# GpSimd's bias adds in the dense stages, moved to VectorE at the head of each trip of the edge sums

## The chip, the cores and the metric

The kernel runs on one core of a Trainium2 chip, in one launch. The metric is the device time of that core in microseconds. Engines are named as the profile does: PE is TensorE (PEld its weight loads), DVE is VectorE, ACT is ScalarE, POOL is GpSimd, SP is SyncE.

## The reference

A graph network on N = 3125 nodes with D = 256 features and 50000 edges. Eight layers follow each other, each x = x + f(layernorm(x)), where f is in turn a sparse sum, a mixture of experts, two graph attention layers, experts, a graph convolution with a small MLP, experts, two SAGE layers, experts. Cut to the four places where the change adds something:

```python
# L1_gnn: two attention layers; the second ends with "+ b2" (gat2)
h1 = relu(gat_conv(x, src, dst, W1, att_src1, att_dst1, b1, n))
out = gat_conv(h1, src, dst, W2, att_src2, att_dst2, b2, n)
# L2_gnn: sum over edges, then an MLP whose second bias is b2 (gcn2)
h7 = segment_sum(msgs, row_sl) + b
out = relu(h7 @ W1 + b1) @ W2 + b2
# L3_gnn: two SAGE layers with biases b1 (sage1) and b2 (sage2)
def _sage_conv(x, src, dst, W_l, b_l, W_r):
    mean_nb = segment_sum(take(x, src), dst) / maximum(deg, 1)
    return mean_nb @ W_l + b_l + x @ W_r
h = _sage_conv(relu(_sage_conv(x, src, dst, W1_l, b1, W1_r)), src, dst, W2_l, b2, W2_r)
```

## The kernel before

The nodes lie in 25 row tiles of 128 (NT = 25). X, in SBUF, holds the running x as [128, NT, 256] in f32; acc holds the result of an edge sum in the same layout with some columns more; TR holds the part of a SAGE layer that comes from the node itself (x @ W_r).

A layer on the graph is made of two kinds of stage. `dense(...)` is a stage between sums: for each group of row tiles (`FIVES` is five groups of 5 tiles, `SHORT_END` is 5, 5, 5, 5, 3, 2) VectorE takes over what came before (`front`, or rows that land from the experts, `got`), makes the layernorm (`stats`, and `finish`, whose L865 writes the normalised rows XN), TensorE transposes the rows and multiplies them with a weight, ScalarE copies the products, and SyncE stores a table in DRAM. `edge_sum(...)` then gathers rows of that table, one of 128 edges per instruction, on GpSimd (L1063, an indirect DMA); VectorE builds a 0/1 matrix S for each 128 edges (L1153, L1155), TensorE multiplies S with the gathered rows G into a product buffer psM (L1138), and VectorE adds that product to the row tile of acc to which these edges belong (`add_up`, L1169). The loop over edge tiles runs on each engine by itself, with semaphores between them: 26 trips of 16 tiles in the sums of this text. At the head of a trip VectorE loads the 16 tile numbers from SBUF into registers (L1199) and computes semaphore thresholds (L1166). The ring of G has 4 groups of 4 tiles, so the gathers run ahead of the rest.

The stages in order, as far as they matter here: gat2's sum (2051 to 2600 us), the dense stage of ffn1 (to 2666), experts; gcn's sum (2946 to 3495), the dense stage of gatf (to 3589); later the dense stage of sage1, sage1's sum (4670 to 5204), the dense stage of sage2, sage2's sum, the dense stage of ffn3. A dense stage is one block: all engines meet at its end (L642).

GpSimd, which has no other work in a dense stage but a maximum over partitions in some, adds there what doesn't come out of a matmul. With `pool_front` it starts at the block's start and VectorE waits for it group by group (semaphore `pooled`): in ffn1 it adds the row gat2 to X (L1806), in gatf the row gcn2 to X (L1827), 5 instructions of 128x1280 each. With `pool_back` it waits until a group's products have been copied (semaphore `kept`): in sage1 it adds the row sage1 to TR (L1886) and the row sage2 to X (L1887), in sage2 TR to X (L1890). In ffn1 VectorE's `front` is L1734, acc times the reciprocal of the denominators, and L1793, X plus acc; in gatf its first operations are L849.

## Time and profile before

| | |
|---|---|
| median of 3 runs | 6393.6 us (6387.85 to 6398.09) |
| the profiled execution, its own time | 6414.7 us |
| its span, mean granted TensorE clock | 6413.0 us, 0.815 |
| busy: PE, DVE, ACT, POOL | 4584.1 (71%), 3483.9 (54%), 2388.4 (37%), 3812.5 (59%) us |

Busy us of the engines by stage, from the windows of the trace:

| stage | window, us | PE | DVE | ACT | POOL | clock |
|---|---|---|---|---|---|---|
| gat2's sum | 2051 to 2600 | 431.29 | 321.79 | 497.34 | 405.76 | 0.83 |
| dense, ffn1 | 2600 to 2666 | 30.46 | 43.77 | 11.56 | 17.97 | 0.50 |
| gcn's sum | 2946 to 3495 | 411.13 | 470.66 | 279.41 | 403.09 | 0.98 |
| dense, gatf | 3495 to 3589 | 74.96 | 44.61 | 35.53 | 16.60 | 0.84 |
| dense, sage1 | 4566 to 4667 | 58.30 | 51.00 | 26.03 | 29.30 | 0.78 |
| sage1's sum | 4670 to 5204 | 309.62 | 270.08 | 20.10 | 394.96 | 0.76 |
| dense, sage2 | 5206 to 5268 | 52.56 | 15.87 | 23.76 | 14.45 | 0.92 |

A row of the groups by line reads: line, engine, operation, what is written from what, shapes, count; then busy time and mean duration in ns; then the idle time of the engine just before these instructions, with what ended it and how much of the idle time each ended. "issue" is an end that the profile shows no cause for. The clock is the share of TensorE's full clock that was granted.

### The profile page before, as it was taken

To read this page: it belongs to the slowest core of one execution; us is meant where nothing else is said; L and a number is where in the kernel's file an instruction comes from. 1 tells how busy PE (TensorE), PEld (TensorE's weight loads), DVE (VectorE), ACT (ScalarE), POOL (GpSimd) and SP (SyncE) were. 2 spreads that over 40 slices of the span, in tenths; PEclk is the share of its full clock that TensorE was granted. 3 is DMA by queue.
4 is the path that set the end of the run, shared out by engine and by line. 5 is a ranking of instruction groups with operands and counts; after the bars stand their busy time and mean duration, and the time that the engine had idled before them with its cause. 6 is when DMAs were issued, how large, how long until landed. Compare 5 with 4: busy or idle time off the path is not lost. (4 is left out here: it accounts for less than half of the span.)

```text
span 6413.0 us, 102638 instructions
## 1 busy us (share of the span) xinstructions
PE 4584.1 (71%) x20814; PEld 3576.9 (56%) x20815; DVE 3483.9 (54%) x11701; ACT 2388.4 (37%) x8150; POOL 3812.5 (59%) x3882
## 2 busy tenths in 40 slices
PE   3846664967887887477777888868755565556997
PEld 1434443756666666465555788867533433335876
DVE  7877876245554555638887444452455445554012
ACT  0745540228997999224554211112200010001221
POOL 4757751756775777364776477754377747771221
PEclk8989986988887888698999655559877777776998
DMA  2023332133333333333333111122233333333555
GB/s 54 1 83 103 103 89 78 58 89 99 106 106 85 106 106 106 79 102 119 103 104 75 23 8 8 8 22 78 85 95 105 105 76 105 105 105 99 178 175 172
DMA packets 303001, 562.12 MB, mean 88 GB/s; under 512 B 87704, under 2 KB 181570, under 8 KB 302530
## 3 DMA queue, kind: packets, MB, share of 16 engines
q0 software_dynamic: 169952, 401.65, 25.0%
q1 hardware_dynamic: 119852, 146.38, 7.1%
q10 hardware_dynamic: 13110, 13.08, 0.6%
q8 instruction: 36, 0.59, 0.0%
q14 instruction: 51, 0.42, 0.0%
HBM read 491.05 MB, written 69.80 MB: 87 GB/s over the span
## 5 line engine op out<-in xcount | busy, mean ns | idle before, releaser
L1138 PE MATMUL psM<-G,S 128*128 128x257 f32 (+3 forms) x6080 | 1939.8, 456 | 998.3 <-DMA G<-table_ones,ids 604.2
L1138 PEld LDWEIGHTS psM<-G,S 128*128 128x128 f32 x6080 | 1329.4, 251 | 1426.3 <-DVE acc L1169 640.8
L1169 DVE TENSOR_TENSOR acc<-acc,psM 128x257 f32 (+3 forms) x3068 | 1151.2, 375 | 1012.5 <-PE psM L1138 820.5
L1063 POOL DMA_INDIRECT G<-table_ones,ids x1248 | 1196.9, 959 | 430.3 <-issue 355.4
L1063 POOL DMA_INDIRECT G<-table_gat,ids x840 | 811.8, 966 | 266.1 <-issue 255.1
L1021 ACT ACTIVATE G<-G 128x64 f32<-128x64 f32 x3360 | 824.7, 333 | 6.8
L1063 POOL DMA_INDIRECT G<-table_ffn_gat,ids x548 | 522.5, 954 | 176.2 <-issue 141.5
L1517 POOL DMA_INDIRECT out_by_choice<-ys,to_choice x248 | 248.6, 1002 | 526.7 <-DVE ys L1637 471.2
L1637 DVE TENSOR_TENSOR ys<-psY,b2b 128x256 f32<-128x256 f32 x248 | 105.2, 425 | 801.1 <-PE psY L1576 744.3
L1063 POOL DMA_INDIRECT G<-table_gcn,ids x416 | 402.5, 968 | 197.1 <-issue 125.6
L1090 PEld LDWEIGHTS psE<-AD,St 128*128 128x128 f32 x2800 | 504.2, 260 | 27.1 <-issue 6.3
L1576 PE MATMUL psY<-w2s,Ht 128*128 (+1 forms) x2240 | 504.0, 379 | 0.0
L1100 PE MATMUL psV<-Ot,Pk 128*128 128x272 f16 (+1 forms) x2496 | 483.3, 303 | 0.0
L1090 PE MATMUL psE<-AD,St 128*128 x2800 | 479.5, 299 | 4.6 <-ACT St L1014 4.6
L1610 ACT ACTIVATE Ht<-psH,b1t 128x256 f32<-128x256 f32 x560 | 260.8, 474 | 584.9 <-PE psH L1564 584.3
L1010 ACT CAST ids<-id_by_dst 128x4 int32 (+1 forms) x428 | 78.6, 185 | 1032.1 <-PE psM L1138 1006.9
L1576 PEld LDWEIGHTS psY<-w2s,Ht 128*128 128x128 f32 x2240 | 426.3, 190 | 58.6 <-issue 0.4
L1153 DVE TENSOR_SCALAR S<-iota_row,dl_by_dst 128x128 f32<-128x128 f32 x1712 | 450.2, 296 | 2.1 <-issue 0.5
L1512 POOL DMA_INDIRECT XN<-rows_by_token,from_token x184 | 179.5, 975 | 357.0 <-POOLq L1277 301.9
L1081 PE MATMUL psS<-ident,S 128*128 128x128 f32 x1400 | 292.0, 346 | 78.9 <-DVE S L1153 74.0
L1100 PEld LDWEIGHTS psV<-Ot,Pk 128*128 128x128 f16 x2496 | 247.5, 99 | 141.4 <-issue 6.3
L1178 DVE TENSOR_TENSOR z<-G,psE 128x16 f32<-128x16 f32 x347 | 59.3, 171 | 478.7 <-DMA G<-table_ffn_gat,ids 265.5
(380 smaller groups left out, 6570.3 us busy)
## 6 DMA issues: line engine op xcount, KB each, us to landing
w1s<-in_L_ffn_W SPq DMA_DIRECT2D x32, 1024.0 KB, 8.5
w2s<-in_L_ffn_W SPq DMA_DIRECT2D x32, 1024.0 KB
G<-table_ones,ids POOLq DMA_INDIRECT x1248, 2.8
land<-out_by_choice SPq DMA_DIRECT2D x75, 256.0 KB, 3.1
G<-table_gat,ids POOLq DMA_INDIRECT x840
rows_by_token<-XN SPq DMA_DIRECT2D x20, 640.0 KB, 3.3
G<-table_ffn_gat,ids POOLq DMA_INDIRECT x548, 2.4
G<-table_gcn,ids POOLq DMA_INDIRECT x416
```

What stands on the lines that cost most here:

```text
L1021: m = nc.scalar.activation(part, part, ACT.Copy, scale=G[:, g, j, HEADS * c + h:HEADS * c + h + 1])
L1063: pool.indirect_dma_start(G[:, g, j, :], None, table, bass.IndirectOffsetOnAxis(ids[:, g, j:j + 1], 0)).then_inc(gathered[g], 16)
L1081: m = nc.tensor.transpose(psS[:, k0 % 2, j * P:(j + 1) * P], S[:, g, j, :], ident[:, :])
L1090: m = nc.tensor.matmul(psE[:, k0 % 2, j, :], St[:, g, j, :], AD[:, bass.ds(bl[j], 1), :].rearrange("p a h -> p (a h)"), start=True, stop=True)
L1100: m = nc.tensor.matmul(psV[:, k, v, 0:HW], Pk[:, ring, k, :], Ot[:, ring, v * HW:(v + 1) * HW], start=False, stop=False)
L1138: nc.tensor.matmul(psM[:, j, 0:W], S[:, g, j, :], G[:, g, j, :], start=True, stop=True).then_inc(summed, 1)
L1153: m = nc.vector.tensor_scalar(S[:, k0 % GB, j, :], iota_row[:, :], DL[:, t], None, ALU.is_equal)
L1169: nc.vector.tensor_tensor(ab, ab, psM[:, n0 % EG, 0:W], ALU.add).then_inc(added, 1)
L1512: pool.indirect_dma_start(xs[:, n % XR, h, :], None, XD, bass.IndirectOffsetOnAxis(from_token[:, n * HALVES + h:n * HALVES + h + 1], 0)).t ...
L1517: pool.indirect_dma_start(YD, bass.IndirectOffsetOnAxis(to_choice[:, n * HALVES + h:n * HALVES + h + 1], 0), ys[:, n % 2, h, :], None).the ...
L1576: m = nc.tensor.matmul(psY[:, q, 0:D], Ht[:, s, h, q * P:(q + 1) * P], w, start=(h == 0), stop=(h == nh - 1))
L1610: nc.scalar.activation(Ht[:, s, h, :], psH[:, h % 2, 0:TT], func, bias=b1t[:, bass.ds(e, 1), h:h + 1].rearrange("p a h -> p (a h)")).then_ ...
```

## The change

`pool_front`, `pool_back` and `pooled` go from `dense`, and with them the 27 additions that GpSimd made in the dense stages (5 in ffn1, 5 in gatf, 12 in sage1, 5 in sage2). `edge_sum` gets a parameter `each`: on VectorE, at the head of each of the 26 trips, behind the load of the 16 tile numbers and ahead of the first group, `each(i)` adds to row tile i. In gat2's sum it adds the row gat2 to tile i of X, in gcn's the row gcn2 to tile i of X, in sage1's the row sage1 to tile i of TR and the row sage2 to tile i of X, in sage2's tile i of TR to tile i of X: 26, 26, 52 and 26 instructions of 128x256. As there are 26 trips and 25 tiles, X and TR get a 26th tile that nobody reads; GpSimd zeroes it in X at the start, and VectorE in TR at the head of sage1's sum (`zeros_beside`).

```diff
@@ def dense
-                        if pool_front is not None:
-                            for t0, t1 in groups:
-                                pool_front(t0, t1).then_inc(pooled, 1)
-                        if beside is not None:
-                            beside(pool)
-                        if pool_back is not None:
-                            for t0, t1 in groups:
-                                pool.wait_ge(kept, t1)
-                                pool_back(t0, t1).then_inc(pooled, 1)
...
                             if front is not None:
-                                if pool_front is not None:
-                                    dve.wait_ge(pooled, g + 1)
                                 m = front(link, t0, t1)
@@ def edge_sum
                                 skip_runtime_bounds_check_because="the chip clamps the block to the last one")
+                            if each is not None:
+                                each(i)
                             for g in range(GB):
@@
+        def tile_of(v, i):
+            return v[:, bass.ds(i, 1), :].rearrange("p a d -> p (a d)")
+
+        def add_to(v, w):
+
+            return nc.vector.tensor_tensor(v, v, w, ALU.add)
@@ gat2's sum and ffn1
-            edge_sum("gat2", LB, tabg[1], WGAT, acc, self_terms(XN, own, acc, 64), AD=AD, c=64)
-
-            def add_gat2(t0, t1):
-                return nc.gpsimd.tensor_tensor(X[:, t0:t1, :], X[:, t0:t1, :], wide(row["gat2"][:, :], t1 - t0), ALU.add)
-            dense("ffn1", FIVES, xn_row, fold=denominators, front=divided_into_x, pool_front=add_gat2, small=(wgt["gate1"], 8, LG, []), tables=[(XD, XN, D, "rows")])
+            edge_sum("gat2", LB, tabg[1], WGAT, acc, self_terms(XN, own, acc, 64), AD=AD, c=64,
+                     each=lambda i: add_to(tile_of(X, i), row["gat2"][:, :]))
+            dense("ffn1", FIVES, xn_row, fold=denominators, front=divided_into_x, small=(wgt["gate1"], 8, LG, []), tables=[(XD, XN, D, "rows")])
@@ sage1 and sage2
-            def add_biases(t0, t1):
-                nc.gpsimd.tensor_tensor(TR[:, t0:t1, :], TR[:, t0:t1, :], wide(row["sage1"][:, :], t1 - t0), ALU.add)
-                return nc.gpsimd.tensor_tensor(X[:, t0:t1, :], X[:, t0:t1, :], wide(row["sage2"][:, :], t1 - t0), ALU.add)
-
-            def add_own(t0, t1):
-                return nc.gpsimd.tensor_tensor(X[:, t0:t1, :], X[:, t0:t1, :], TR[:, t0:t1, :], ALU.add)
+            def add_biases(i):
+                add_to(tile_of(TR, i), row["sage1"][:, :])
+                return add_to(tile_of(X, i), row["sage2"][:, :])
+
+            def add_own(i):
+                return add_to(tile_of(X, i), tile_of(TR, i))
+
+            def zeros_beside(acc, W):
+                def begin():
+                    nc.vector.memset(TR[:, NT, :], 0.0)
+                    return nc.vector.memset(acc[:, :, 0:W], 0.0)
+                return begin
@@
-            edge_sum("sage1", LB, tab1[1], W1TAB, acc, zeros_in(acc, W1TAB))
+            edge_sum("sage1", LB, tab1[1], W1TAB, acc, zeros_beside(acc, W1TAB), each=add_biases)
-            edge_sum("sage2", LB, tab1[2], W1TAB, acc, zeros_in(acc, W1TAB))
+            edge_sum("sage2", LB, tab1[2], W1TAB, acc, zeros_in(acc, W1TAB), each=add_own)
```

The same is done to gcn's sum and gatf with the row gcn2, and the sizes of X and TR become NT + 1 tiles.

On GpSimd, between the last gathers of gat2's sum and the first gathers of ffn1's experts, there stands before (L1806 is the addition of the row gat2; ISA in front of it is a configuration instruction):

```order
L1063 DMA G<-table_gat,ids 128x260 x4
L993 UNCONDITIONAL_BRANCH
L665 UNCONDITIONAL_BRANCH
L1806 ISA
L1806 TENSOR_TENSOR X<-X,row_gat_1 128x1280 x5
L642 UNCONDITIONAL_BRANCH
L1508 UNCONDITIONAL_BRANCH
L1512 DMA xs<-rows_by_token,from_token 128x256 x10
```

and now, with lines numbered as in the changed kernel:

```order
L1053 REGISTER_ALU
L1053 COMPARE_AND_BRANCH
L1050 DMA G<-table_gat,ids 128x260 x4
L980 UNCONDITIONAL_BRANCH
L665 UNCONDITIONAL_BRANCH
L1497 UNCONDITIONAL_BRANCH
L1501 DMA xs<-rows_by_token,from_token 128x256 x10
```

The configuration instruction and the five additions are gone, and GpSimd passes the dense stage with nothing to do.

On GpSimd in the dense stage of sage1 there stands before, for each group, a pair of additions; this is its beginning, behind the scatters of the experts:

```order
L1477 UNCONDITIONAL_BRANCH
L665 UNCONDITIONAL_BRANCH
L1886 ISA
L1886 TENSOR_TENSOR TR<-TR,row_sage_1 128x1280
L1887 TENSOR_TENSOR X<-X,row_sage_1 128x1280
```

and now the gathers of the sum follow directly:

```order
L1466 UNCONDITIONAL_BRANCH
L665 UNCONDITIONAL_BRANCH
L1046 UNCONDITIONAL_BRANCH
L1053 UNCONDITIONAL_BRANCH
L1053 ISA
L1050 DMA G<-table_ones,ids 128x257 x4
```

All twelve additions have left this place.

On VectorE, at the head of the loop of sage1's sum, there stands before (L1719 zeroes acc, L1169 adds a product to it, L1153 builds S):

```order
L1719 MEMSET acc 128x6425
L1198 UNCONDITIONAL_BRANCH
L1198 ISA
L1199 TENSOR_LOAD blk_by_dst
L1166 REGISTER_ALU
L1167 REGISTER_ALU
L1169 ISA
L1169 TENSOR_TENSOR acc<-acc,psM 128x257
```

and now:

```order
L1885 MEMSET TR 128x256
L1886 MEMSET acc 128x6425
L1185 UNCONDITIONAL_BRANCH
L1185 ISA
L1186 TENSOR_LOAD blk_by_dst
L1712 ISA
L1712 TENSOR_TENSOR TR<-TR,row_sage_1 128x256
L1712 REGISTER_ALU
L1712 TENSOR_TENSOR X<-X,row_sage_1 128x256
L1153 REGISTER_ALU
L1154 REGISTER_ALU
L1156 ISA
L1156 TENSOR_TENSOR acc<-acc,psM 128x257
```

The two additions stand between the load of the tile numbers and the first addition of a product; the threshold registers come behind them.

## Rows read from the trace of the kernel before

**Rows 1.** The groups by line, GpSimd, in gat2's (2051 to 2600), gcn's and sage1's sums.

```profile
L1063 POOL DMA_INDIRECT G<-table_gat,ids x420 | 405.8, 966 | 133.5 <-issue 127.7 <-ACT ids L1010 5.8
...
L1063 POOL DMA_INDIRECT G<-table_gcn,ids x416 | 402.5, 968 | 197.1 <-issue 125.6 <-SPq L993 70.6 <-ACT ids L1010 0.9
...
L1063 POOL DMA_INDIRECT G<-table_ones,ids x416 | 395.0, 949 | 131.0 <-issue 124.7 <-ACT ids L1010 6.3
```

**Rows 2.** The same view, VectorE, in gcn's sum (2946 to 3495).

```profile
L1169 DVE TENSOR_TENSOR acc<-acc,psM 128x256 f32 x420 | 171.7, 409 | 75.9 <-PE psM L1138 75.8
```

**Rows 3.** The timeline of ffn1's dense stage: start us, us, engine, instruction, [idle before].

```profile
2606.14 17.97 POOL L1806 TENSOR_TENSOR X<-X,row_gat 128x1280 f32<-128x1280 f32 x5 [21.59 <-issue]
...
2598.82 0.78 DVE L1784 RECIPROCAL rden<-acc 128x100 f32<-128x100 f32 x1 [1.08 <-PEq L993]
2609.11 4.09 DVE L1734 TENSOR_TENSOR acc<-acc,rden 128x1280 f32<-128x1280 f32 x1 [9.51 <-POOL X L1806]
2613.24 4.05 DVE L1793 TENSOR_TENSOR X<-X,acc 128x1280 f32<-128x1280 f32 x1
...
2619.45 1.93 DVE L1734 TENSOR_TENSOR acc<-acc,rden 128x1280 f32<-128x1280 f32 x1
...
2629.44 1.48 DVE L1734 TENSOR_TENSOR acc<-acc,rden 128x1280 f32<-128x1280 f32 x1
2630.95 1.49 DVE L1793 TENSOR_TENSOR X<-X,acc 128x1280 f32<-128x1280 f32 x1
```

**Rows 4.** The timeline of gatf's dense stage.

```profile
3496.36 6.37 DVE L849 TENSOR_TENSOR acc<-acc,DINV 128x1280 f32<-128x1280 f32 x2
...
3498.78 1.09 PE L687 MATMUL psA<-ident,acc 128*128 128x128 f32 x4 [2.53 <-DVE acc L849]
```

**Rows 5.** The timeline of sage1's dense stage, VectorE.

```profile
4599.29 1.70 DVE L865 TENSOR_SCALAR XN<-X,mv,rstd 128x256 f32<-128x256 f32 x5
...
4610.65 2.95 DVE L865 TENSOR_SCALAR XN<-X,mv,rstd 128x256 f32<-128x256 f32 x5
...
4637.23 2.30 DVE L865 TENSOR_SCALAR XN<-X,mv,rstd 128x256 f32<-128x256 f32 x3
...
4647.53 5.01 DVE L865 TENSOR_SCALAR XN<-X,mv,rstd 128x256 f32<-128x256 f32 x2
```

**Rows 6.** The same stretch, TensorE.

```profile
4601.32 1.88 PE L728 MATMUL psL<-w_sage,xts 128*128 128x512 f32 x4
...
4614.14 3.08 PE L728 MATMUL psL<-w_sage,xts 128*128 128x512 f32 x4
...
4652.60 0.69 PE L719 MATMUL psT<-ident,XN 128*128 128x128 f32 x2 [5.29 <-DVE XN L865]
4653.08 3.62 PE L728 MATMUL psL<-w_sage,xts 128*128 128x512 f32 x4
```

**Rows 7.** The end of sage2's dense stage: GpSimd's timeline, and the last table store.

```profile
5260.41 2.88 POOL L1890 TENSOR_TENSOR X<-X,TR 128x1280 f32<-128x1280 f32 x1 [5.86 <-ACT XN L802]
...
L662 SPq DMA_DIRECT2D table_ones<-XN x1: 360/360/360, 5260.4 to 5260.4; - x1
...
DMA to landing us min/median/max: 4.5/4.5/4.5
```

**Rows 8.** The timeline at the head of gat1's sum.

```profile
1461.04 7.09 DVE L1725 TENSOR_TENSOR acc<-XN,own 128x1280 f32<-128x1280 f32 x5
1461.50 7.45 POOL L1063 DMA_INDIRECT G<-table_gat,ids  x1 [0.30 <-issue]
```

**Rows 9.** Register steps of line L1166, and the gathers that start beside them.

```profile
L1166 DVEq ALU_OP  x1: 40/40/40, 3214.7 to 3214.7; - x1
...
3214.82 0.95 POOL L1063 DMA_INDIRECT G<-table_gcn,ids  x1 [0.30 <-issue]
...
L1166 DVEq ALU_OP  x1: 40/40/40, 4912.4 to 4912.4; - x1
...
4912.46 0.95 POOL L1063 DMA_INDIRECT G<-table_ones,ids  x1 [0.30 <-issue]
```

More of the change, by code:

```diff
@@ L117, in linker @@
             return link
-        X = sb("X", [P, NT, D])
+        X = sb("X", [P, NT + 1, D])
         ident = sb("ident", [P, P])
@@ L460, in _ @@
                         nc.gpsimd.memset(zeros[:, :], 0.0).then_inc(zeroed, 1)
-                        nc.gpsimd.memset(X[:, NT - 1, :], 0.0).then_inc(own, 1)
+                        nc.gpsimd.memset(X[:, NT - 1:NT + 1, :].rearrange("p t d -> p (t d)"), 0.0).then_inc(own, 1)
                         nc.gpsimd.memset(eps[:, :], LN_EPS).then_inc(own, 1)
@@ L593, in dense @@
         def dense(name, groups, rows, ln=True, got=None, front=None, first=None, col=None, W=None, scale=None, into=None,
-                  small=None, tables=(), att=None, fold=None, degrees=None, beside=None, pool_front=None, pool_back=None, also=None):
+                  small=None, tables=(), att=None, fold=None, degrees=None, also=None):
             LAG = 9 if first is not None else 0
@@ L899, in _ @@
                             if front is not None:
-                                if pool_front is not None:
-                                    dve.wait_ge(pooled, g + 1)
                                 m = front(link, t0, t1)
@@ L946, in _, with edge_sum @@
                             nc.vector.tensor_tensor(zo[:, :, :], zo[:, :, :], att.AD[:, :, HEADS:2 * HEADS], ALU.subtract).then_inc(scored, 1)
-        def edge_sum(name, e, table, W, acc, begin, AD=None, c=64, job=None):
+        def edge_sum(name, e, table, W, acc, begin, AD=None, c=64, job=None, each=None):
             with ExitStack() as ctx:
@@ L1823, in program @@
             edge_sum("gcn", LA, tabx, D, acc, lambda: nc.vector.tensor_copy(acc[:, :, :], XN[:, :, 0:D]),
-                     job=Job(LF, LF.by_pool, list_dram[LF.name][0:LF.slots, :]))
-            def add_gcn2(t0, t1):
-                return nc.gpsimd.tensor_tensor(X[:, t0:t1, :], X[:, t0:t1, :], wide(row["gcn2"][:, :], t1 - t0), ALU.add)
+                     job=Job(LF, LF.by_pool, list_dram[LF.name][0:LF.slots, :]), each=lambda i: add_to(tile_of(X, i), row["gcn2"][:, :]))
             def to_x(t, ps):
@@ L1831, in program @@
             dense("gatf", FIVES, xn_row, first=First(acc_row2, acc_group, DINV, column["gcn"], (wgt["gcn1"], column["gcn1"]), wgt["gcn2"], to_x, None),
-                  pool_front=add_gcn2, small=(wgt["gatf"], WF + HEADS, TF, []), att=Att(TF, AD, own, 4), tables=[(XD, XN, D, "rows"), (tabf, TF, WF, "small")])
+                  small=(wgt["gatf"], WF + HEADS, TF, []), att=Att(TF, AD, own, 4), tables=[(XD, XN, D, "rows"), (tabf, TF, WF, "small")])
             edge_sum("gatf", LF, tabf, WF, acc, self_terms(TF, own, acc, 4), AD=AD, c=4)
@@ L1873, in program @@
             sb, pb, sem = scope(ctx)
-            TR = sb("TR", [P, NT, D])
+            TR = sb("TR", [P, NT + 1, D])
             acc = sb("acc", [P, NT, W1TAB])
@@ L1903, in joined_into_x @@
                 return m
-            dense("sage1", SHORT_END, xn_row, got=True, W=(wgt["sage1"], 2 * D), into=own_row, also=xn_row, pool_back=add_biases, tables=[(tab1[1], XN, D, "kept")])
-            edge_sum("sage1", LB, tab1[1], W1TAB, acc, zeros_in(acc, W1TAB))
-            dense("sage2", FIVES, xn_row, ln=False, fold=in_degrees, front=joined, pool_back=add_own,
+            dense("sage1", SHORT_END, xn_row, got=True, W=(wgt["sage1"], 2 * D), into=own_row, also=xn_row, tables=[(tab1[1], XN, D, "kept")])
+            edge_sum("sage1", LB, tab1[1], W1TAB, acc, zeros_beside(acc, W1TAB), each=add_biases)
+            dense("sage2", FIVES, xn_row, ln=False, fold=in_degrees, front=joined,
                   W=(wgt["sage2"], 2 * D), into=own_row, also=xn_row, tables=[(tab1[2], XN, D, "kept")])
-            edge_sum("sage2", LB, tab1[2], W1TAB, acc, zeros_in(acc, W1TAB))
+            edge_sum("sage2", LB, tab1[2], W1TAB, acc, zeros_in(acc, W1TAB), each=add_own)
             dense("ffn3", FIVES, xn_row, fold=in_degrees, front=joined_into_x, small=(wgt["gate3"], 8, LG, [row["gate3"][:, :]]), tables=[(XD, XN, D, "rows")])
```

2 lines of the change are left out of this document (1 added, 1 removed).

## The prediction, made before the changed kernel ran

> **What bounds the kernel now.** The page's list of instructions comes first: no engine is full over the span, so the average decides nothing, and its chain of the work that ended last names no line with a share above 0%. So I read stage by stage, with the groups by line in the windows of the edge sums and with the timeline in the stages between them.
>
> In the sums GpSimd sets the pace. One gather instruction is busy 0.949 to 0.968 us, and nearly all of its idle time is "issue", about 0.30 us each: in the gcn sum 402.5 + 125.6 = 528 us of some 549 [rows 1]. VectorE waits for TensorE's products in the same stretches, 75.9 us in the gcn sum, which is the fullest of the four for it [rows 2]. A trip of a loop is 16 gathers, there are 26 trips, so VectorE has at least 75.9 / 26 = 2.9 us to spare in each. The reader is to see two things: short work on VectorE fits there, and whatever holds a gather lengthens the sum one for one.
>
> In the stages between sums GpSimd does only the five or six adds that the change takes away. In ffn1 VectorE waits for them openly [rows 3]; in sage1 they lie beside VectorE's last step of the layernorm, and that step is longer wherever they do [rows 5].
>
> **What the removed adds are worth, stage by stage.**
>
> ffn1. VectorE finishes the reciprocal at 2598.82 + 0.78, then waits 9.51 us for the first of GpSimd's adds; its own two operations on that group then take 4.09 and 4.05 us, and those on the second 1.93 us and again 4.05 (the row reads like the one shown). Once GpSimd is nearly through, the same operations take 1.48 and 1.49 us [rows 3]. GpSimd itself had not started before 2606.14, after 21.59 us in which nothing that the profile shows held it [rows 3]: the configuration instruction ahead of its first add fills the last part of that. Adds and instruction go. So the first four operations shrink by 2.61 + 2.56 + 0.45 + 2.56 = 8.2 us, and the stage starts to deliver normalised rows 9.5 + 8.2 = 17.7 us sooner. What is late next is VectorE itself, whose groups pace the rest of the stage as before, and TensorE behind it; I take all 17.7. If something else ended the stage it would be less (a rival).
>
> gatf. The adds of X stand in time before VectorE needs them. They do stretch VectorE's first two operations to 6.37 us for the pair, and TensorE starts its transposes at 3498.78, 2.42 us after the first began [rows 4]. At ffn1's undisturbed 1.48 us [rows 3] it would start 0.9 us earlier. From there TensorE has the lead. I take 0.9 (0 to 2).
>
> sage1. The step L865 is 1.70 us for a group of five where GpSimd is idle, and 2.95 us where it adds; the next group of five takes 2.93 us (a row like it), the one of three 2.30 us and that of two 5.01 us [rows 5]. By 0.34 us a tile the undisturbed times are 1.70, 1.70, 1.02 and 0.68, so the excess is 1.25 + 1.23 + 1.28 + 4.33 = 8.1 us. It is on the path: TensorE waits for just this step, 5.29 us before the last group [rows 6], longer than the excess of 4.33 us, and 2.0 to 2.7 us before the three others, longer than theirs. Behind the waits TensorE is slower: its four matmuls take 3.08 and 3.62 us instead of 1.88 us [rows 6]; 3.62 is near twice 1.88, the lower of the clock's two levels (1.2 and 2.4 GHz) against the upper. With shorter waits part of that may go: 0 if it falls anyway, 1.2 + 1.7 + about 2 for the third place and the last group's rest, say 5, if it never falls. I take 3. The tail: GpSimd's last add ends a little after the last table store was issued; 0.2 us. Sum 11.3 (8 to 13.5).
>
> sage2. The last of its adds is 2.88 us from 5260.41, and the last table store goes out at 5260.4 and lands 4.5 us later, which the stage waits for anyway [rows 7]. Gain 0. If that cover were gone, 2.88 would be the most.
>
> Sum of gains: 17.7 + 0.9 + 11.3 + 0 = 29.9 us (between 26 and 34).
>
> **What the added ones cost.** There are 26 + 26 + 52 + 26 = 130 adds of 128x256 on VectorE. The trace has no such instruction with both sources in SBUF; by 1.48 us for 1280 columns [rows 3], and by 0.41 us for the 256-column addition of a product into acc [rows 2], it takes 0.41 us, or less when two stand together. Per trip that is 0.41 us, in sage1's sum some 0.8, against at least 2.9 us of slack [rows 2]. At a trip's head the adds stand ahead of the first group's additions into acc, for which TensorE waits before it reuses a product buffer; since GpSimd's gathers are what TensorE waits for, this is covered. If it were not, 130 x 0.41 = 53 us would be on the path (a rival). The 128x256 memset of TR at the head of sage1's sum stands before one of 128x6425; it is 4% of that work and lies beside gathers already under way, so nothing. The same for the larger memset of X at the start, and for the configuration and clearing instructions that change their places.
>
> What is not covered is a collision. At the head of gat1's sum a run of VectorE additions with two SBUF sources (7.09 us) lies beside a gather that takes 7.45 us instead of 0.95: it began 0.46 us after the run did and ended 0.82 us after it [rows 8]. So such an addition seems to hold a gather's work until it is over. Of a gather that starts in the middle, 0.95 - 0.82 = 0.13 us is done before it is held. Then a single add of 0.41 us holds a gather by 0.28 us at most, a pair (about 0.75 us) by 0.62 us. Gathers follow each other every 1.25 us. By chance, a single add catches a gather's start in 0.28 / 1.25 = 22% of trips and costs 0.14 us on the mean, a pair in 50% and 0.31: 78 x 0.22 x 0.14 + 26 x 0.50 x 0.31 = 6.4 us. If every trip collides fully it is 78 x 0.28 + 26 x 0.62 = 38 us. Which holds depends on where in a gather the trip's head falls. In the one head of the gcn sum that I read VectorE reaches its step L1166, where the add would stand, at 3214.7 and a gather starts at 3214.82; in sage1's it is 4912.4 and 4912.46 [rows 9]. Both are full collisions, but two heads are few, and a trip's head shifts against the gathers as each held gather moves the next. I take 12 us, nearer to chance than to always, and keep 0 and 38 as the ends.
>
> **By the rule and by the row.** The row has a gather of 7.45 us beside five two-source additions [rows 8]. The Trainium skill, "SBUF — State Buffer", section "Who interferes with whom", says that a tensor_tensor with both inputs in SBUF takes only the read side of the port pair that VectorE shares with GpSimd, and infers that descriptor generation, which needs the write side, is not held. By that rule the added work costs nothing, and the sum is the full 29.9. The trace does not agree with it here, so the sum goes by the row.
>
> **The sum.** 29.9 - 12 = 17.9 us saved. The profiled execution took 6414.7 us (span 6413.0, and 1.7 us around it), so it would be about 6397. The median of the runs shown is 6393.6, 21 us below that execution; nothing in the sum depends on which is used, so I take it off the median: 6393.6 - 18 = 6375. A change under 0.2%, some 13 us, is about what a measurement of this kernel cannot tell from none.
>
> **The rivals.**
> No hold at all. A gather beside a short two-source addition runs on, and the 7.45 us came from the size or number of those operations. Speaks for it: each add is a quarter as long as those in the row. Against it: that gather lasts just as long as the run. Time 6393.6 - 29.9 = 6364. Chance 0.17.
> Collisions in most trips. The two heads that I read would be typical, because after a held gather the pace settles into the same place each trip. Cost 17 to 38 us, at the end 29.9 - 38 = +8, 6402; for most of it the result is within 0.2%. Chance 0.20.
> The gain in ffn1 is given back. If what ends the stage did not depend on VectorE's front, only about 12 would be left of the gains, all eaten by collisions: 6394. Against it: VectorE waits at the very start, with TensorE idle behind it [rows 3]. Chance 0.04.
> Slower. The adds at the head of a trip stand on the path, since TensorE's next product waits for the addition into acc behind them. All 130 would then cost 53 us, 53 - 29.9 = +23, about 6417; with 43 us or more it is slower by over 0.2%. It decides only if VectorE had less slack per trip than an add is long, and it has 2.9 against 0.41 [rows 2]. Chance 0.04.
>
> **How the numbers follow.** Forecast (part of the trips collide) 0.55, with its own range 6366 to 6384: gains 26 to 34 less a cost of 6 to 17. Faster by over 0.2%: 0.55 + 0.17, and a little of the third case's lower end: 0.73. Within 0.2%: 0.19 + 0.04: 0.23. Slower: 0.04. The range from 6361 takes in the case of no hold, and up to 6388 the lower half of the case of many collisions; outside stand some 0.10 of that case and the last two, 0.18.
>
> **What would show it.** In the trace of the changed kernel: in ffn1, VectorE's L1734 (its line there is lower) right after the reciprocal, with no 9.5 us wait, 1.48 us from the first, and the stage some 18 us shorter; in sage1, the layernorm step at 1.70, 1.70, 1.0 and 0.7 us, with TensorE's waits shorter; the new adds at 0.41 us; and in the four sums gathers of 1.1 to 1.6 us where an add lies beside them, in sage1's most (half of the 12 us over its 416 gathers would raise their mean from 949 to some 963 ns). The prediction is wrong if the gathers beside adds stay at 0.95 us (then it is near 6364), or if each trip's first gather is longer (then near 6395).

## The result

| | before | changed |
|---|---|---|
| median of 15 runs | 6393.01 us | 6377.72 us (6372.05 to 6384.86) |
| ratio, 95% interval | | 0.9976 [0.9968, 0.9984] |
| span of the profiled execution, clock | 6413.0 us, 0.815 | 6376.0 us, 0.816 |

The kernel is 15.3 us faster (10 to 20 by the interval); forecast were 18. The two profiled executions differ by 37 us, more than the medians. Some 10 us of that lie in the set-up, which the change hardly touches: the first gather starts at 385.8 us in the execution before and at 375.9 in the changed kernel's. The set-up's 167 indirect scatters had a mean of 1230 ns before, 1147 in the changed kernel's and 1096 to 1189 in every later one, also of kernels that differ from before by one instruction (b_tiny_behind_zeros 1170). So single spans aren't compared below; stages are.

The first lines of the profile's page of the changed kernel, its span and the busy time of each engine:

```profile
span 6376.0 us, 102860 instructions
...
PE 4573.1 (72%) x20814; PEld 3569.0 (56%) x20815; DVE 3507.6 (55%) x11832; ACT 2388.9 (37%) x8150; POOL 3732.1 (59%) x3855
```

GpSimd has 27 instructions and 80 us less, of which the set-up's scatters are 14 and the removed additions 78; the held gathers that follow below give some back. VectorE has 131 instructions more (130 additions and a memset).

ffn1's dense stage, the timeline of VectorE, to be read beside [rows 3]:

```profile
2586.28 0.78 DVE L1780 RECIPROCAL rden<-acc 128x100 f32<-128x100 f32 x1 [1.08 <-PEq L980]
2587.10 1.49 DVE L1730 TENSOR_TENSOR acc<-acc,rden 128x1280 f32<-128x1280 f32 x1
2588.62 1.49 DVE L1789 TENSOR_TENSOR X<-X,acc 128x1280 f32<-128x1280 f32 x1
...
2592.28 1.46 DVE L1730 TENSOR_TENSOR acc<-acc,rden 128x1280 f32<-128x1280 f32 x1
2593.77 1.49 DVE L1789 TENSOR_TENSOR X<-X,acc 128x1280 f32<-128x1280 f32 x1
...
2599.24 1.48 DVE L1730 TENSOR_TENSOR acc<-acc,rden 128x1280 f32<-128x1280 f32 x1
```

The wait of 9.51 us is gone, and the four stretched operations take 1.46 to 1.49 us. From the reciprocal's start to the third group's L1730 it is 12.96 us; in [rows 3] it was 30.62. That is 17.66 us, the 17.7 of the prediction.

gatf's dense stage, the timeline, beside [rows 4]:

```profile
3463.47 2.89 DVE L840 TENSOR_TENSOR acc<-acc,DINV 128x1280 f32<-128x1280 f32 x2
...
3465.10 1.09 PE L678 MATMUL psA<-ident,acc 128*128 128x128 f32 x4 [1.74 <-DVE acc L840]
```

TensorE starts 1.63 us behind VectorE's first operation instead of 2.42: 0.8 us.

sage1's dense stage, the timeline of VectorE and then of TensorE, beside [rows 5, 6]:

```profile
4575.26 1.71 DVE L856 TENSOR_SCALAR XN<-X,mv,rstd 128x256 f32<-128x256 f32 x5
...
4597.96 1.06 DVE L856 TENSOR_SCALAR XN<-X,mv,rstd 128x256 f32<-128x256 f32 x3
...
4605.32 0.73 DVE L856 TENSOR_SCALAR XN<-X,mv,rstd 128x256 f32<-128x256 f32 x2
...
4577.29 1.88 PE L719 MATMUL psL<-w_sage,xts 128*128 128x512 f32 x4
...
4606.11 0.44 PE L710 MATMUL psT<-ident,XN 128*128 128x128 f32 x2 [1.01 <-DVE XN L856]
4606.39 1.88 PE L719 MATMUL psL<-w_sage,xts 128*128 128x512 f32 x4
```

The layernorm step has its short times, TensorE's wait before the last group is 1.01 instead of 5.29 us, and its four matmuls take 1.88 us there and at the other places where they took 3.08 and 3.62. With the shorter waits the clock did not fall: its mean is 1.00 from 4560 to 4615 us, where in the kernel before it was 0.90 from 4596 to 4665 us.

The new additions and what they do to the gathers: the groups by line, first VectorE, then GpSimd in gcn's, sage1's and sage2's sums, beside [rows 1]:

```profile
L1712 DVE TENSOR_TENSOR X<-X,row_gat 128x256 f32 x26 | 11.1, 425 | 32.7 <-issue 32.7
L1712 DVE TENSOR_TENSOR X<-X,row_gcn 128x256 f32 x26 | 11.6, 445 | 16.2 <-issue 16.2
...
L1050 POOL DMA_INDIRECT G<-table_gcn,ids x416 | 404.1, 971 | 196.0 <-issue 126.4 <-ACT ids L997 69.6
...
L1050 POOL DMA_INDIRECT G<-table_ones,ids x416 | 401.3, 965 | 214.2 <-issue 124.9 <-ACT ids L997 89.3
...
L1050 POOL DMA_INDIRECT G<-table_ones,ids x416 | 402.3, 967 | 204.2 <-issue 124.3 <-ACT ids L997 79.9
```

An addition takes 0.42 to 0.45 us. In sage1's sum the gathers are busy 401.3 us, 6.3 more than in [rows 1]. Most of that is not spread over the trips as the prediction had it. The timeline of the head of sage1's sum, and then of sage2's:

```profile
4622.54 6.62 POOL L1050 DMA_INDIRECT G<-table_ones,ids  x1 [0.30 <-issue]
4622.66 5.41 DVE L1886 MEMSET acc<- 128x6425 f32 x1 [1.29 <-issue]
...
4627.99 0.36 DVE L1712 TENSOR_TENSOR TR<-TR,row_sage 128x256 f32 x1
...
5226.74 7.65 POOL L1050 DMA_INDIRECT G<-table_ones,ids  x1 [0.30 <-issue]
5227.89 5.41 DVE L1715 MEMSET acc<- 128x6425 f32 x1 [1.29 <-issue]
...
5233.21 0.36 DVE L1712 TENSOR_TENSOR X<-X,TR  x1
```

One gather in each sum takes 6.62 and 7.65 us. It ends 0.82 us after the first addition of the loop has ended (5233.21 + 0.36 + 0.82 = 5234.39 = 5226.74 + 7.65; for the other 4627.99 + 0.36 + 0.82 = 4629.17, and 4622.54 + 6.62 = 4629.16). Yet it starts 5.45 and 6.47 us before that addition. That is what the experiments are about.

### The profile page after: what moved, and what is told of

Read it like the earlier page. It is cut to its first block and busy times, and to the rows that moved or that the text cites. A ratio compares the mean times of both kernels' runs of the same rounds, so it can differ in the third digit from the quotient of the medians.

```text
span 6376.0 us, 102860 instructions
## 1 busy us (share of the span) xinstructions
PE 4573.1 (72%) x20814; PEld 3569.0 (56%) x20815; DVE 3507.6 (55%) x11832; ACT 2388.9 (37%) x8150; POOL 3732.1 (59%) x3855
## 5 line engine op out<-in xcount | busy, mean ns | idle before, releaser
L1050 POOL DMA_INDIRECT G<-table_ones,ids x1248 | 1210.4, 970 | 589.6 <-issue 357.1
L1050 POOL DMA_INDIRECT G<-table_gcn,ids x416 | 404.1, 971 | 196.0 <-issue 126.4
```

Of the source, the lines that this page charges most:

```text
L1050: pool.indirect_dma_start(G[:, g, j, :], None, table, bass.IndirectOffsetOnAxis(ids[:, g, j:j + 1], 0)).then_inc(gathered[g], 16)
```

## The experiments

All on a chip like that of the first runs, unless said. The table gives, from the traces, the time from the first gather's start to the last gather's end of three sums.

| kernel | gcn's | sage1's | sage2's | ratio to before, interval |
|---|---|---|---|---|
| before | 529.0 | 521.5 | 521.1 | |
| changed | 530.5 | 527.7 | 528.7 | 0.9976 [0.9968, 0.9984] |
| a_zeros_first | 530.9 | 528.2 | 527.6 | 0.9982 [0.9973, 0.9992] |
| a_sage_sums_bare (78 additions left out) | 530.5 | 520.4 | 520.6 | 0.9956 [0.9939, 0.9972] |
| b_tiny_behind_zeros | 528.3 | 520.8 | 520.5 | 0.9998 [0.9989, 1.0008] |
| b_gat2_only | 526.5 | 521.0 | 520.7 | 0.9976 [0.9966, 0.9986] |
| a_adds_at_trip_end | 527.6 | 522.4 | 521.5 | 0.9964 [0.9953, 0.9975] |
| a_end_and_own_on_pool | 534.7 | 522.5 | 520.8 | 0.9960 [0.9947, 0.9974] |
| p_add256_add24 | 527.3 | 526.9 | 520.2 | one run |
| p_scalar25_scalar128 | 528.4 | 520.9 | 526.9 | one run |
| c_gat2_and_sage1_again | 528.1 | 521.7 | 520.8 | 0.9952 [0.9939, 0.9966] |

**a_zeros_first.** In sage1's and sage2's sums the zeroing of acc (`begin`) is issued ahead of the S instructions:

```diff
+                        if begin_first:
+                            begin().then_inc(added, EG)
                         for k in range(AHEAD):
                             for j in range(EG):
                                 make_s(None, k, j)
-                        begin().then_inc(added, EG)
+                        if not begin_first:
+                            begin().then_inc(added, EG)
```

> The changed kernel, but in sage1's and sage2's sums the zeroing of acc stands ahead of the twelve S instructions, so that no addition with two SBUF sources is next in line behind it. Theory A (such an addition, once it is next in line behind a long VectorE instruction, already shuts gathers out, so that the one gather of 6.62 and the one of 7.65 us at the heads of these sums come from the addition that waits behind the zeroing): both shrink to 0.95 us or, beside a short wait, under 1.7 us; both sums 5 to 7 us shorter than in the changed kernel (527.7 and 528.7 us between first and last gather), the kernel about 12 us below the changed one, ratio to before near 0.9957. Rival B (the zeroing itself shuts out a gather when the two meet in this phase): long gathers of over 5 us stay beside the zeroing. Rival C (the cost of the sums is spread over the 26 trips): sums change by under 2 us.

Measured: nothing gained. The head of sage2's sum, the timeline:

```profile
5230.23 6.56 POOL L1050 DMA_INDIRECT G<-table_ones,ids  x1 [77.10 <-ACT ids L997]
5230.49 5.41 DVE L1718 MEMSET acc<- 128x6425 f32 x1 [1.29 <-issue]
...
5235.81 2.34 DVE L1140 TENSOR_SCALAR S<-iota_row,dl_by_dst 128x128 f32<-128x128 f32 x12
```

The long gather is there although the addition is 12 instructions away. Theory A as written fell, and rival B seemed to hold; but the gather ends at 5236.79, which is 0.82 us after 5235.97, about where the first of the 12 S instructions ends (a single one takes 0.16 us in the probe below). That left open that any instruction next in line that needs what GpSimd needs is enough.

**a_sage_sums_bare.** The two sums without their 78 additions:

```diff
-            edge_sum("sage1", LB, tab1[1], W1TAB, acc, zeros_beside(acc, W1TAB), each=add_biases)
+            edge_sum("sage1", LB, tab1[1], W1TAB, acc, zeros_beside(acc, W1TAB))
...
-            edge_sum("sage2", LB, tab1[2], W1TAB, acc, zeros_in(acc, W1TAB), each=add_own)
+            edge_sum("sage2", LB, tab1[2], W1TAB, acc, zeros_in(acc, W1TAB))
```

> The changed kernel without the 78 additions in sage1's and sage2's sums: it leaves out both SAGE biases and the second layer's own part. It gives the whole cost of the added work there. Theory A: the sums fall back to about 521.5 us between first and last gather, 6.2 and 7.6 us below the changed kernel, with no gather over 1.3 us; ratio to before near 0.9955. If the additions cost VectorE's path and not only gathers, the sums fall below 521 us or the dense stages behind them start sooner than that by more.

Measured: 520.4 and 520.6 us, 7.3 and 8.1 less than in the changed kernel, no gather over 1.05 us. The zeroing stands in the same place, and gathers start in the same spots beside it as the two long ones did, 0.12 us ahead of it in sage1's sum and 1.14 us in sage2's (0.12 and 1.15 in the changed kernel). The zeroing alone holds nothing: rival B is out.

**b_tiny_behind_zeros.** The kernel before, with

```diff
+            def zeros_and_tiny():
+                nc.vector.memset(acc[:, :, 0:W1TAB], 0.0)
+                return nc.vector.tensor_tensor(rdeg[:, :], iota_row[:, 0:NT], ident[:, 0:NT], ALU.add)
```

as `begin` of sage1's and sage2's sums.

> The kernel before, with one tiny addition more in each of sage1's and sage2's sums: 128x25 from two SBUF sources, about 0.1 us long, right behind the zeroing of acc (its result is overwritten later, nothing of the computation changes). Theory A: one gather at the head of each sum lasts until that addition is over, 5 to 7.7 us instead of 0.95, and each sum is 5 to 7 us longer than before; the kernel 10 to 13 us slower, ratio 1.0018. Rivals B and C, and the prediction's own view (a gather is held only while such an addition runs): no change, each gather at most 1.1 us.

Measured: no effect. In sage2's sum, the timeline:

```profile
5250.33 5.41 DVE L1893 MEMSET acc<- 128x6425 f32 x1 [1.29 <-issue]
5250.45 0.95 POOL L1063 DMA_INDIRECT G<-table_ones,ids  x1 [0.30 <-issue]
...
5255.65 0.12 DVE L1894 TENSOR_TENSOR rdeg<-iota_row,ident 128x25 f32<-128x25 f32 x1
```

A second miss for theory A, this time with an addition of two SBUF sources next in line, but of 25 columns. The two probes below take this apart.

**p_add256_add24 and p_scalar25_scalar128.** As before, with another instruction behind the zeroing, in sage1's sum and in sage2's:

```diff
+                return nc.vector.tensor_tensor(TR[:, NT, :], row["sage1"][:, :], row["sage2"][:, :], ALU.add)
+                return nc.vector.tensor_tensor(TR[:, NT, 0:24], iota_row[:, 0:24], ident[:, 0:24], ALU.add)
...
+                return nc.vector.tensor_scalar(TR[:, NT, 0:25], iota_row[:, 0:25], 1.0, None, ALU.add)
+                return nc.vector.tensor_scalar(TR[:, NT, 0:128], iota_row[:, :], 1.0, None, ALU.add)
```

> The kernel before with one harmless instruction more right behind the zeroing of acc: in sage1's sum an addition of 128x256 from two SBUF sources into an unused tile, in sage2's one of 128x24. The tiny one of 128x25 held nothing. If size or an even count decides, the 128x256 holds a gather for over 5 us and the 128x24 shows which of the two it is (held: an even count; not held: the size). If neither holds, it is not the addition but that it stands in the loop, behind the instruction that computes its address.

> The kernel before with one harmless tensor_scalar more right behind the zeroing of acc: in sage1's sum 128x25 from one SBUF source, in sage2's 128x128 like those that build S. In the kernel with the zeroing first, a gather was held until the first S instruction behind the zeroing was over, so the 128x128 should hold one gather over 5 us; the 128x25 holds none if an even count or size decides.

Measured: the addition of 256 columns and the tensor_scalar of 128 hold a gather, those of 24 and 25 columns hold none. The timelines, first of p_add256_add24 at the head of sage1's sum:

```profile
4652.10 7.41 POOL L1063 DMA_INDIRECT G<-table_ones,ids  x1 [0.30 <-issue]
4653.01 5.41 DVE L1894 MEMSET acc<- 128x6425 f32 x1 [1.18 <-issue]
...
4658.33 0.36 DVE L1899 TENSOR_TENSOR TR<-row_sage 128x256 f32<-128x256 f32 x1
```

and of p_scalar25_scalar128 at the head of sage2's:

```profile
5252.85 7.43 POOL L1063 DMA_INDIRECT G<-table_ones,ids  x1 [0.31 <-issue]
5253.98 5.41 DVE L1894 MEMSET acc<- 128x6425 f32 x1 [1.29 <-issue]
...
5259.31 0.16 DVE L1902 TENSOR_SCALAR TR<-iota_row 128x128 f32<-128x128 f32 x1
```

The second gather began 1.13 us before the zeroing started and 6.46 us before the instruction that held it, which works for 0.16 us. Both sums are 6 us longer, from one harmless instruction. The place of the gather isn't the reason: in sage2's sum of b_tiny_behind_zeros and of p_add256_add24 a gather also begins 1.13 us ahead of the zeroing, and takes 0.95 us. Theory A stands with a correction: it depends on the instruction next in line, and one of few columns doesn't hold. For the tensor_scalar the source is the same in both probes, so the count alone decides between 25 and 128 columns; whether its size or its being odd was not tried. The additions differ in their sources too. That 64 columns are enough for an operation with two sources in SBUF is in the trace of the kernel before, in gatf's sum (L1208 multiplies G with a part of G):

```profile
4096.42 1.18 POOL L1063 DMA_INDIRECT G<-table_ffn_gat,ids  x1 [0.30 <-ACT ids L1010]
...
4096.56 0.22 DVE L1208 TENSOR_TENSOR G<-G 128x64 f32<-128x64 f32 x1
```

The gather ends 0.82 us after L1208 has, which starts only 0.14 us after it.

**a_adds_at_trip_end.** `each(i)` stands behind the loop over groups instead of ahead of it:

```diff
-                            if each is not None:
-                                each(i)
                             for g in range(GB):
...
                                             place(i * U + (g * EG + EG + j), (g + 1) % 2 * EG + j)
+                            if each is not None:
+                                each(i)
```

> The changed kernel with the same 130 additions, at the end of each trip instead of its head. So the instruction next in line behind the zeroing of acc is the first addition of a product, which waits for TensorE. Theory A (the instruction next in line behind a long one already shuts gathers out if it uses what GpSimd needs): no long gather at the head of sage1's and sage2's sums; between first and last gather 523 to 524 us each instead of 527.7 and 528.7; the 1.6 to 1.8 us per sum that are spread over the trips stay; kernel 9 to 11 us below the changed one, ratio to before 0.996. Rival D (the hold of 5 to 7 us comes from the meeting of the zeroing with a gather in a certain phase, whatever follows): long gathers stay in one sum at least.

Measured: as expected. 522.4 and 521.5 us, a little better than forecast, and 0.9964 [0.9953, 0.9975]. The two sums are 12.5 us shorter than in the changed kernel; by the ratios alone, whose intervals overlap a little, the gain on it is 8 us. The timeline of the head of sage2's sum:

```profile
5218.83 5.41 DVE L1715 MEMSET acc<- 128x6425 f32 x1 [1.29 <-issue]
5218.93 0.94 POOL L1050 DMA_INDIRECT G<-table_ones,ids  x1 [0.30 <-issue]
...
5224.38 0.42 DVE L1156 TENSOR_TENSOR acc<-acc,psM 128x257 f32 x1
```

The instruction next in line now waits for TensorE's product and has one of its sources in PSUM, and the gathers run through the zeroing. This run doesn't tell the two apart. That such an addition holds nothing while it runs is in every sum: in sage1's sum of the kernel before, some 80 gathers start while one runs, and none of them takes more than 0.95 us.

**a_end_and_own_on_pool.** The same, with sage2's own part back on GpSimd:

```diff
+                        if pool_back is not None:
+                            for t0, t1 in groups:
+                                pool.wait_ge(kept, t1)
+                                pool_back(t0, t1)
```

> As the kernel with the additions at the trips' end, but the own part of the second SAGE layer is added by GpSimd in sage2's dense stage, as before the change (5 additions of 128x1280). By the prediction's term for sage2 (2.88 us of the last addition under a store that lands 4.5 us later) that stage is not longer, and sage2's sum loses its 1.6 to 2 us of held gathers and falls to 521 us: 1.5 us below the kernel with all additions at the trips' end. If the GpSimd additions had cost something there that the prediction missed (VectorE has little to do in that stage), the stage is 1 to 3 us longer and the two cancel.

Measured: 0.9960, not told apart from 0.9964. sage2's sum falls by 0.7 us instead of 1.6 to 2, and the time from sage1's sum to sage2's is 78.4 us against 76.6, where no difference was expected. Other traces of this stretch lie between 75.2 and 78.0 us, so this pair does not settle what the addition costs on GpSimd. But gcn's sum, whose code is the same in both, takes 534.7 us here and 527.6 there. The timeline at the end of a trip of gcn's sum in this kernel:

```profile
2978.56 0.35 DVE L1153 TENSOR_SCALAR Ot<-iota,tile_by_ffn_dst 128x544 f16<-128x544 f16 x1
2978.58 1.48 POOL L1054 DMA_INDIRECT G<-table_gcn,ids  x1 [0.31 <-issue]
...
2978.83 0.41 DVE L1716 TENSOR_TENSOR X<-X,row_gcn 128x256 f32 x1
```

The addition stands behind an operation of 0.35 us, a gather starts with it, and is held until 0.82 us after the addition's end: 0.53 us, longer than the 0.28 us that the addition alone could hold. There are eight such gathers in this sum, seven of them in successive trips, and two in the same sum of a_adds_at_trip_end. That is about half of the 7 us between the two sums. The other half is no addition at all: the operation of 0.35 us by itself, L1153 here and L1162 in the kernel before, holds 44 gathers here and 26 there. Which gathers fall into such a spot differs from execution to execution, so a difference of a few us in gcn's sum says little.

**b_gat2_only.** The kernel before with `each` in gat2's sum, and without `pool_front` in ffn1.

> The kernel before with one part of the change alone: the row gat2 is added on VectorE in gat2's sum, the other additions stay on GpSimd. By the prediction's terms ffn1's dense stage is 17.7 us shorter and gat2's sum 0 to 2 us longer: ratio to before 0.9972. In the changed kernel's trace gcn's first gather came 20.1 us sooner against gat2's last one than before; if that is the change and not the scatter between executions, the same is seen here.

Measured: 0.9976 [0.9966, 0.9986], 15 us, all of the change's net gain by itself. From gat2's sum to gcn's it takes 342.2 us, as in the changed kernel (341.5); gat2's sum takes 533.6 us, before 533.5.

**c_gat2_and_sage1, b_sage1_at_trip_end, c_changed_again.** The first is the kernel before with the additions of gat2 and of the two SAGE biases on VectorE at the end of each trip, and those of gatf and sage2 left on GpSimd; the second has the SAGE biases alone.

```diff
-            dense("sage1", SHORT_END, xn_row, got=True, W=(wgt["sage1"], 2 * D), into=own_row, also=xn_row, pool_back=add_biases, tables=[(tab1[1], XN, D, "kept")])
-            edge_sum("sage1", LB, tab1[1], W1TAB, acc, zeros_in(acc, W1TAB))
+            dense("sage1", SHORT_END, xn_row, got=True, W=(wgt["sage1"], 2 * D), into=own_row, also=xn_row, tables=[(tab1[1], XN, D, "kept")])
+            edge_sum("sage1", LB, tab1[1], W1TAB, acc, zeros_beside(acc, W1TAB), each=add_biases)
```

> The kernel before with two parts of the change alone, those whose GpSimd additions cost something: the row gat2 in gat2's sum and the two SAGE biases in sage1's sum, at the end of each trip. The additions of gatf and of sage2 stay on GpSimd. From the traces so far: ffn1 18 us less, sage1's dense stage 15 us less, sage1's sum 1 us more, the rest as before, so about 32 us below before, ratio 0.995, and as good as or better than the kernel with all additions at the trips' end (0.9964). If gatf's stage gains more than gcn's sum pays, this kernel is 1 to 3 us behind that one.

> The kernel before with the two SAGE biases alone moved to VectorE, at the end of each trip of sage1's sum. By the prediction's terms the dense stage gains 8.1 us where the layernorm step is no longer stretched, 3 us (0 to 5) by TensorE's clock and 0.2 us at the end; by the trace of the changed kernel it is 15 us. Ratio to before 0.9977 by the trace, 0.9983 by the terms.

> The changed kernel itself once more, beside the two others on the same chip: ratio 0.9976 as measured; it gives a second trace of it, to tell the change from the scatter between executions: long gathers of over 5 us at the heads of sage1's and sage2's sums again, those sums at 527 to 529 us, TensorE at its upper clock throughout sage1's dense stage.

Measured, on another chip on which before takes 7615.84 us: 0.9961 [0.9945, 0.9977], 0.9978 [0.9963, 0.9993] and 0.9974 [0.9961, 0.9986]. Absolute times aren't comparable with the others. The instructions of the gathers in c_changed_again, in sage1's sum and in sage2's (ns min/median/max, first and last start):

```profile
L1050 POOL DMA_INDIRECT G<-table_ones,ids x416: 943/949/6616, 5648.8 to 6284.0; - x139
...
L1050 POOL DMA_INDIRECT G<-table_ones,ids x416: 943/949/7644, 6362.1 to 6995.4; - x139
```

The two long gathers are there again, 6.616 and 7.644 us against 6.616 and 7.647 in the first trace: they belong to the kernel, not to an execution. TensorE's clock is up there too, 1.00 from 5588 to 5645 us in sage1's dense stage. The sums themselves take 636 and 634 us: GpSimd waits 195.2 us in sage1's sum for ScalarE's ids, against 89.3 us in the first trace, and the DMA engines move 86 GB/s in it against 103. As the ids follow the ring, this points to the arrival of the rows as what paces it; that was not tried. The expectation of 527 to 529 us didn't hold for that reason, and the forecast of 0.995 for the two parts is not settled by this run.

**c_gat2_and_sage1_again.** The same kernel on a chip like that of the other runs.

> The kernel with two parts of the change alone once more, since its first run fell on a chip on which every kernel takes about 7600 us. On a chip like that of the other runs, where gathers are issued every 1.25 us in the sums: ffn1 18 us less, sage1's dense stage 15 us less, sage1's sum 1 us more, ratio to before 0.995 to 0.996, the same as or better than with all additions at the trips' end.

Measured: 6361.62 us against 6391.94, 0.9952 [0.9939, 0.9966]: 30 us faster than before, and below the changed kernel's interval. It is the lowest ratio of the complete kernels, but its interval overlaps those of a_adds_at_trip_end (0.9964) and a_end_and_own_on_pool (0.9960), so that leaving two parts alone gains anything over moving all four to the trips' end is not shown. Its sums are those of before to within a microsecond.

## Why the prediction was right

The traces give each stage in several kernels with and without its part of the change. Between two sums the time is that from one's last gather to the next one's first; it takes in what stands between them beside the dense stage, the experts for one.

| stage | GpSimd adds | moved | change | predicted |
|---|---|---|---|---|
| gat2's sum to gcn's (ffn1) | 359.4 to 361.7, mean of four 360.6 | 340.9 to 343.6, of seven 342.0 | -18.6 | -17.7 |
| gcn's sum to gatf's | 113.6 to 116.9, of six 114.8 | 111.2 to 113.7, of five 112.7 | -2.1 | -0.9 |
| gatf's sum to sage1's | 389.1 to 392.2, of five 391.2 | 376.0 to 378.4, of six 376.8 | -14.4 | -11.3 |
| sage1's sum to sage2's | 75.2 to 76.6, of five 76.1 (and 75.4) | 76.6 to 78.0, of four 77.4 | +1.3 | 0 |
| gat2's sum | | | 0 | 12 in all four |
| gcn's sum | 526.5 to 529.0 | 530.5 to 530.9 (at the head) | +2.7 | |
| sage1's sum | 520.8 to 521.5 | 527.7, 528.2 (at the head) | +6.9 | |
| sage2's sum | 520.2 to 521.1 | 528.7, 527.6 (at the head) | +7.5 | |

Gained are 18.6 + 2.1 + 14.4 - 1.3 = 33.8 us, paid in the sums 2.7 + 6.9 + 7.5 = 17.1, net 16.7, against 15.3 by the medians. In the prediction they were 29.9, 12 and 17.9.

**ffn1** was right in mechanism and size: the wait and the four stretched operations, 17.66 us by the rows, and b_gat2_only gives 15 us (9 to 22) on the clock for that part alone. Nothing of it is given back.

**gatf** was right, 0.8 of the 0.9 us in its first operations. The other 1.3 us of the stage and the +1.3 us between sage1's and sage2's sums are where semaphores are cleared (L81): three clearing steps left the end of gatf's dense stage and three that of sage1's, four now stand behind gatf's sum and five behind sage1's. They were put at nothing, which holds for their sum to within a microsecond or two. Between sage1's and sage2's sums a_sage_sums_bare, without any addition, has 78.0 us, so the 1.3 us are not the additions; a_end_and_own_on_pool, with the clearing as in the changed kernel but GpSimd's additions back in sage2, has 78.4 us, and the two-part kernel, with the clearing as before, 75.4. That the clearing is what the 1.3 us are is argued from the order and these, not tried alone. In sage1's dense stage it doesn't show: the two-part kernel keeps its three steps there and has 376.3 us all the same.

**sage1's dense stage** was right in mechanism and undersized: the excess of 8.1 us in the layernorm step went, and the clock term, taken as 3 (0 to 5), came out above its upper end. From the first group's L865 to the issue of the last table store it takes 75.05 us before and 60.54 in the changed kernel, 14.5 less; without the 8.1 that leaves 6.4 for TensorE's work. The clock no longer fell in the middle of the stage, and in the first group, which the term left out, the first eight matmuls take 3.04 and 1.88 us instead of 3.62 and 2.17. By the table it is 14.4 us against 11.3; b_sage1_at_trip_end has a ratio of 0.9978 [0.9963, 0.9993], which fits both.

**sage2** at 0: the stage with GpSimd's additions takes 75.2 to 76.6 us and without them no less, which fits the reading of [rows 7] that the store covers them. The one trace against it is a_end_and_own_on_pool with its 78.4 us.

**The cost** was in its range by luck: the 12 us (0 to 38) became 17, most of it by another mechanism than that priced. And the total was right because two misses cancel: the gains were 4 us larger than forecast, and the cost 5. The collisions within the trips cost 0.8 to 1.4 us in each of sage1's and sage2's sums (522.4, 522.5 and 521.5 with the additions at the trips' end against 521.1 and 520.7; in the changed kernel 6.9 and 7.5 less the 5.7 and 6.7 of the one long gather). Gather by gather, where each long one is put down to the VectorE instruction that ended 0.82 us before it did, the additions of the changed kernel lengthen 1 gather in gat2's sum, 11 in gcn's and, without the two long ones, 12 in sage1's and 10 in sage2's, by 0.2, 2.9, 1.7 and 1.7 us: 6.5 us, next to the 6.4 that the prediction had worked out by chance before it took 12. The step "a single add of 0.41 us holds a gather by 0.28 us at most" was right where the addition is alone. For a pair it had 0.62 us; none was held by over 0.25, since the hold ends with the first addition although the second follows at once, as in sage1's sum of the changed kernel:

```profile
4688.38 1.08 POOL L1050 DMA_INDIRECT G<-table_ones,ids  x1 [0.30 <-issue]
...
4688.22 0.42 DVE L1712 TENSOR_TENSOR TR<-TR,row_sage 128x256 f32 x1 [1.24 <-issue]
4688.56 0.42 DVE L1712 TENSOR_TENSOR X<-X,row_sage 128x256 f32 x1
```

The gather ends 0.82 us after the first addition, 4689.46 us, and not after the second. In [rows 8] it is otherwise: that gather was held through five additions in a row. Why these differ is open. Single additions, in the timeline of the changed kernel, one trip's head in gat2's sum and one in gcn's:

```profile
2094.57 0.95 POOL L1050 DMA_INDIRECT G<-table_gat,ids  x1 [0.30 <-issue]
...
2094.91 0.43 DVE L1712 TENSOR_TENSOR X<-X,row_gat 128x256 f32 x1 [1.27 <-issue]
...
2999.22 1.19 POOL L1050 DMA_INDIRECT G<-table_gcn,ids  x1 [0.30 <-issue]
...
2999.16 0.42 DVE L1712 TENSOR_TENSOR X<-X,row_gcn 128x256 f32 x1 [0.64 <-issue]
```

The first addition begins 0.34 us into the gather and does nothing to it; the second begins 0.06 us ahead of it and costs 0.24 us. What the prediction missed is the head of the sum. It read [rows 8] as "such an addition seems to hold a gather's work until it is over" and counted the hold from the addition's start. The hold also covers the time in which the addition is next in line and does not run yet. So the step that failed is "a single add of 0.41 us holds a gather by 0.28 us at most", for the first trip: there the addition stands behind the zeroing of 5.41 us, and one gather in each of the two sums is held by 5.7 and 6.7 us. That is 12.4 us; with the 6.5 within the trips it makes 18.9 by gathers, against 17.1 by the lengths of the sums, in which other held gathers vary as well.

**The rivals.** "No hold at all" is settled in between. Every gather that was held ended 0.82 us after an instruction of VectorE, so a gather of 0.95 us can be held only in its first 0.13 us; the 0.82 us that follow no addition touches, as in gat2's sum, where the additions fall inside the gathers and all 26 of them lengthen one gather, by 0.15 us. In sage1's and sage2's the hold is real. The Trainium skill, "SBUF — State Buffer", section "Who interferes with whom", has both halves: a two-source instruction contends with what GpSimd reads, and descriptor generation is inferred to be free of it. The trace agrees if the first 0.13 us are a read and the 0.82 us the generation, which no run here shows; that the gather as a whole is free does not follow, as 6.62 and 7.65 us show. "Collisions in most trips" did not come: in the changed kernel it is 11 of 26 trips in gcn's sum, 13 in sage1's and 11 in sage2's, and in a_end_and_own_on_pool, the longest gcn sum, 9. "The gain in ffn1 is given back" is out by the 342.2 us of b_gat2_only. "Slower" did not come: with 52 additions in sage1's sum at the trip's end it is 1 us longer, and GpSimd's idle time between its gathers there is the same 126.4 us with and without additions.

## What to carry to other kernels

Short work can be moved from an engine that another waits for into the slack of a loop, if that slack is read per trip; here 130 additions cost VectorE's path nothing that shows. Then look at what stands ahead of each moved instruction: a two-source SBUF addition of 256 columns (or a tensor_scalar of 128 in SBUF) queued behind a long VectorE instruction shut GpSimd's gathers out until it was over, so put it behind one that waits for a product; that turned 15 us into 24. And move the parts that were in somebody's way: of the four places here two gave nearly all of the gain, and with those two alone at the trips' end it was 30 us, though the step from 24 to 30 is not clear of the noise.

## What the runs showed of the hardware

- A gather that is held ends 0.82 us after the instruction that held it, in every case shown (6.62, 7.65, 7.41, 7.43, 6.56, 1.48, 1.18 and 1.08 us long).
- VectorE's claim begins when the instruction is next in line, up to 6.5 us before it starts, and also while the one ahead has not started (the idle "issue" of 1.29 us ahead of the zeroing). Behind the first of two such additions, and behind the first of twelve tensor_scalar, the gather went on; behind the first of five additions of 128x1280 it did not.
- 128x256 and 128x64 from two SBUF sources and a 128x128 tensor_scalar claim; an addition of 128x24 or 128x25 and a tensor_scalar of 128x25 don't; an addition with one source in PSUM doesn't, nor does a memset.
- Between chips the kernel before took 6392 and 7616 us. Gathers have the same duration on the second (0.949 us median), but in sage1's sum GpSimd waits 195.2 us for its ids instead of 89.3; the changed kernel's ratio agrees (0.9974 and 0.9976).
